# First attention of a two-layer network: scores a whole unit ahead, two blocks sharing a piece, key and query projections joined

## The chip, the core and the metric

The kernel runs on one core of a Trainium2 chip. The core has a matmul engine (TensorE, PE in the profile), three engines for elementwise work (VectorE or DVE, ScalarE or ACT, GpSimd or POOL) and a queue engine (SyncE or SP) that issues DMAs here. All of them run their own instruction streams and meet only at semaphores. The metric is the time of one execution on the device, in microseconds (us); smaller is better.

## What is computed

The reference is a network of two layers on an input x of 8 batch entries, 512 positions and 256 features, all in float32. Each layer is x + mixer(norm(x)) * silu(feed-forward(norm(x))). The change lies in the mixer of the first layer, a causal attention with linear biases: 16 heads of keys and values, two query heads to each, 64 features a head.

```python
qkv = inputs @ W_qkv
q = ...reshape(B, S, 32, 64)            # two query heads for each of the 16 key heads
k, v = ...reshape(B, S, 16, 64), each repeated for its two query heads
bias = ALIBI_SLOPES[:, None, None] * (pos[None, :] - pos[:, None])
scores = einsum('bhqd,bhkd->bhqk', q, k) / sqrt(64) + bias
scores = where(pos_q >= pos_k, scores, -inf)
attn = softmax(scores, axis=-1)
out = einsum('bhqk,bhkd->bhqd', attn, v).reshape(B, S, 2048)
return out @ W_out
```

The feed-forward part, the second layer (a recurrence, another attention, routed experts) and the norms are not touched.

## The kernel before

The whole is one program. `layernorm_phase` comes first and `head_attention_phase` after it (it takes the stretch from about 55 to 1515 us), then the first layer's feed-forward network, the recurrence, the second attention, the routing and the experts. Only `head_attention_phase` is changed.

Its work is cut into units. A unit is one batch entry (B = 8) of one key head (KVH = 16) with its two query heads, so there are 128 units; `t` counts them, and `par` is `t` modulo 2. The 512 positions are four blocks of 128 (TT = 4). By causality, block qt of the queries needs qt + 1 blocks of keys, so scores are 128, 256, 384 or 512 wide. Products in full precision are made of operands split into a high and a low part, in three terms (high by high, low by high, high by low).

PE's work for a unit, with its function and line:

- `project` (L970): six matmuls of 512 columns over 128 rows for keys and values together (`project_kv`), and six for the two query heads (`project_q`), into the banks `m_ps`.
- `turn_v` (L986): four small transposes of v.
- `score` (L1031): for each block six matmuls over 64 rows, two heads side by side in two halves of the array, into the two banks `s_ps`.
- `turn` (L1042): for each block the transposes of the weights p, 4 (qt + 1) pieces over 64 rows, into two banks `t_ps`.
- `weigh` (L1052): the sum over v, 16 matmuls over 128 rows (the four blocks of keys, of 512, 384, 256 and 128 columns), into `o_ps`.
- `project_out` (L997): two times three matmuls of 512 columns (the halves m of the output), into `m_ps`.

The other engines, for each unit:

- DVE: `mask` (L894) adds the bias to a block's score of one head, u = 2 * block + head, takes it out of `s_ps` and finds the row's limit; `invert` (L900) takes reciprocals of the sums; `turn_out` (L905) copies half of the turned weights; `values` (L886) copies v; `k_rest` (L881), `q_rest` (L874) and `rest_o` (L916) compute the low parts; `add_out` (L912) adds the output to `acc`.
- ACT: `exps` (L815) the exponential of a block and head; `turn_out` (L821) the other half of the turned weights; `take_kv` (L808, L809), `take_q` (L801) and `take_o` (L827) the high parts.
- POOL: `scale` (L767) multiplies the exponentials by the reciprocals; once a head it splits new weights (L758, L760).
- SP: `copy_k` (L710) copies the split key by two DMAs of 256 KB each from `k_parts` (64 partitions) into both halves of `k_twice[par]`, and counts them in `k_copied[par]`.

The order is written out by hand in four functions called `body`, one for each engine, and in `body` of PE it is, for block qt of 0 to 3 in unit t:

1. `score` of the block that is three blocks ahead (AHEAD0 = 6 counts block and head, so qt = 0 scores block 3 of unit t, and qt = 1 to 3 score blocks 0 to 2 of unit t + 1); in its last term it waits until block qt of unit t has been scaled (`turnable`).
2. `turn(qt)`.
3. A piece of 128 rows: after qt = 0 `turn_v` of unit t + 1 and `weigh` of unit t - 1; after qt = 1 `project_kv` of unit t + 2; after qt = 2 `project_out` of unit t - 1; after qt = 3 `project_q` of unit t + 2.

DVE, ACT and POOL follow the same blocks. The waits that PE's `body` makes are put where a matmul of the piece before still runs. The key copy of unit t + 1 is waited for in `weigh` of body t (`operands`); it comes from the projection in body t - 1. The low part of the attention's output is waited for in `project_out` (`o_low`), one piece and a block after `weigh`.

Of the kernel before, what the change touches and what calls it, by code (L numbers as in the profile page):

```python
# [597 lines left out]
def head_attention_phase(nc, w_heads, wo_heads, slopes, ident, xh, xl, acc, xh_dram, xl_dram, row_sb, coef_sb,  # L598
# [9 lines left out]
    with ExitStack() as ctx:  # L608
# [65 lines left out]
        AHEAD0 = 6  # L674
# [4 lines left out]
        def ahead(t, qt):  # L679
            return (t, 2 * qt + AHEAD0) if qt < TT - AHEAD0 // 2 else (t + 1, 2 * qt + AHEAD0 - 2 * TT)  # L680

        def soon(t, qt):
            return (t, qt + 2) if qt + 2 < TT else (t + 1, qt + 2 - TT)
# [4 lines left out]
        def q_count(n):  # L688
            return n * 5
# [4 lines left out]
        def out_count(n, m):  # L694
            return n * 5 + (13 + m)
# [53 lines left out]
        def _(pool):  # L749
# [12 lines left out]
            def scale(t, qt):  # L762

                wait_alone(pool, recips, t * TT + (qt + 1), pool_ticks)
                for u in (2 * qt, 2 * qt + 1):
                    p = p_sb[:, u, 0:(qt + 1) * P]
                    pool.tensor_scalar(p, p, recip[:, u:u + 1], 1.0, ALU.mult, ALU.mult).then_inc(scaled, 1)  # L767

            def body(t):
                for qt in range(TT):  # L770
                    scale(*soon(t, qt))
# [5 lines left out]
            with pool.Fori(0, KVH // 2) as jj:  # L777
                for jp in range(2):
# [3 lines left out]
                    pool.wait_ge(proj, j * (5 * B) + out_count(-1, 1))  # L782
# [14 lines left out]
        def _(act):  # L797
# [13 lines left out]
            def exps(n, u):  # L811

                N = (u // 2 + 1) * P
# [4 lines left out]
            def turn_out(n, qt, par):  # L818

                act.wait_ge(turned, n * TT + (qt + 1))  # L820
                act.activation(pT[par][:, :, 0:qt + 1, qt * P + HD:qt * P + P], turned_half(1)[:, :, 0:qt + 1, :],  # L821
                               ACT.Copy).then_inc(odd_out, 1)
# [10 lines left out]
            for u in range(AHEAD0):  # L833
                exps(0, u)
            with act.Fori(0, KVH * B // 2) as pair:
                for par in range(2):
                    t = pair * 2 + par
                    for qt in range(TT):
                        n, u = ahead(t, qt)
                        if qt == 0:  # L840
                            take_q(q_count(t + 1), 1 - par)
                        exps(n, u)
                        turn_out(t, qt, par)
                        exps(n, u + 1)
                        if qt == 0:
                            take_o(t, 1 - par)
                        if qt == 1:
                            take_kv(kv_count(t + 2), par, pair + par)
            take_o(KVH * B, 1)
            take_q(q_count(KVH * B + 1), 1)  # L850

        @block.vector
        def _(dve):
# [35 lines left out]
            def mask(n, u):  # L889


                N = (u // 2 + 1) * P
                wait_alone(dve, scored, n * 8 + (u + 1), dve_ticks)
                dve.tensor_tensor_reduce(out=p_sb[:, u, 0:N], in0=s_ps[u % 2][:, 0:N],  # L894
# [3 lines left out]
            def invert(n, qt):  # L898
                dve.wait_ge(exped, n * 8 + (2 * qt + 2))
                dve.reciprocal(recip[:, 2 * qt:2 * qt + 2], total[:, 2 * qt:2 * qt + 2]).then_inc(recips, 1)  # L900

            def turn_out(n, qt, par):

                dve.wait_ge(turned, n * TT + (qt + 1))
                dve.tensor_copy(pT[par][:, :, 0:qt + 1, qt * P:qt * P + HD], turned_half(0)[:, :, 0:qt + 1, :])\  # L905
# [12 lines left out]
            def body(t, par, b_before, new_head=None):  # L918

                for qt in range(TT):  # L920
                    n, u = ahead(t, qt)
                    if u == 0 and new_head is not None:

                        dve.wait_ge(masked, t * 8 + 10)
                        set_bias(new_head, False, new_head * 2 + 2)
                    if qt == 3:
                        add_out(t + (-1), 1 - par, b_before, 0)
                    if qt == 0:
                        q_rest(t + 1, 1 - par)
                    mask(n, u)  # L930
                    invert(*soon(t, qt))
                    mask(n, u + 1)
                    turn_out(t, qt, par)
                    if qt == 1:
                        values(v_count(t + 1), 1 - par)
                        rest_o(t, 1 - par)
                    if qt == 2:
                        k_rest(t + 2, par)
                    if qt == 3:
                        add_out(t + (-1), 1 - par, b_before, 1)  # L940
# [6 lines left out]
            for u in range(AHEAD0):  # L947
                mask(0, u)
# [8 lines left out]
            q_rest(KVH * B + 1, 1)  # L957
            rest_o(KVH * B, 1)

            for m in range(KT):  # L960
                add_out(KVH * B - 1, 1, B - 1, m, skipped=2)

        @block.tensor
        def _(pe):
            def project(bank, w, b):

                terms = [(wh, xh), (wl, xh), (wh, xl)]
                for i, (weight, x) in enumerate(terms):
                    for k in range(KT):
                        ins = pe.matmul(bank[:], weight[:, k, w:w + P], x[:, k, ds(b * S, S)],  # L970
# [3 lines left out]
            def project_q(n, par, b):  # L974

                pe.wait_ge(proj_out, q_count(n) + (-2))
                project(m_ps[1 - par], 0, b)

            def project_kv(n, par, b):
                pe.wait_ge(proj_out, kv_count(n) + (-2))  # L980
                project(m_ps[par], P, b)
# [1880 lines left out]
```

## Time and profile before

| | us |
|---|---|
| median of three runs | 3470.98 |
| lowest, highest | 3469.5, 3473.81 |
| the profiled execution, its own time | 3471.95 |
| its span in the trace | 3470.2 |
| PE busy in the span | 3213.3 (93%) |
| DVE, ACT, POOL busy | 2348.2 (68%), 2064.0 (59%), 1184.7 (34%) |
| granted TensorE clock over the span, share of full | 0.96 |

The page of the profile gives busy times and the costliest groups. The timeline gives instructions in order of time, and neighbours of a kind merged to one row: the start, the length from there to the end of the last, the engine, the line, the operation, output<-inputs, the shape and the count. An idle note in brackets tells how long the engine was idle before the row, and what it waited for. As matmuls are pipelined, a row's length reaches into the next row, so the time that a piece holds PE is read from its start to the start of the next piece. PEld is PE's loading of weights, which can run beside a matmul. Each operand of a matmul is written as rows*columns.

### The profile page before, as it was taken

The numbers are of one execution on the slowest core, as the hardware profiler recorded it, in microseconds if no ns is written. First come the engines' busy times: TensorE is split into PE (matmuls) and PEld (weight loads), VectorE is DVE, ScalarE is ACT, GpSimd is POOL, SyncE is SP. The second block draws the span as 40 slices with busy tenths as digits, with TensorE's granted clock in tenths as the row PEclk, the third lists the DMA queues.
The fourth block names the chain that finished last, engine by engine and source line by source line (L and its number), as shares of the span: only waits on it lengthen the run. The fifth ranks groups of instructions, "written<-read, shape, count | busy, mean of one in ns | idle before, by whom it ended". The sixth has DMA issues, their size and how long they took to land. (4 is left out here: it accounts for less than half of the span.)

```text
span 3470.2 us, 74087 instructions
## 1 busy us (share of the span) xinstructions
PE 3213.3 (93%) x22696; PEld 2398.4 (69%) x22696; DVE 2348.2 (68%) x6849; ACT 2064.0 (59%) x4943; POOL 1184.7 (34%) x1818
## 2 busy tenths in 40 slices
PE   4999999999999999989999979979999964999995
PEld 3777777676777677768888865546666653888884
DVE  5888887887888788776666655556666626666664
ACT  4777777777777777765555543236566621555553
POOL 4434344444333434443333320042321202334432
PEclk9999999999999999999999999969999967999998
DMA  3222222222222222243333331111111134445545
GB/s 95 59 54 59 52 51 57 59 58 54 59 59 54 58 59 57 55 136 121 131 127 127 133 121 49 39 40 28 32 28 27 27 123 148 118 125 143 128 120 164
DMA packets 175948, 280.43 MB, mean 81 GB/s; under 512 B 32850, under 2 KB 117586, under 8 KB 175826
## 3 DMA queue, kind: packets, MB, share of 16 engines
q1 hardware_dynamic: 161234, 258.94, 26.1%
q0 software_dynamic: 14592, 19.93, 3.5%
q8 instruction: 69, 1.13, 0.1%
q14 instruction: 53, 0.43, 0.0%
HBM read 159.79 MB, written 41.16 MB: 58 GB/s over the span
## 5 line engine op out<-in xcount | busy, mean ns | idle before, releaser
L767 POOL TENSOR_SCALAR at_p<-at_p,at_recip 128x128 f32<-128x128 f32 (+3 forms) x1028 | 533.6, 532 | 868.0 <-DVE at_recip L900 868.0
L815 ACT ACTIVATE at_p<-at_p,at_nmax 128x128 f32<-128x128 f32 (+3 forms) x1030 | 573.6, 557 | 336.4 <-DVE at_nmax L894 324.7
L894 DVE CUSTOM_DVE_ANT_0 at_p<-at_s_ps,at_bias 128x128 f32<-128x128 f32 (+3 forms) x1030 | 497.3, 483 | 208.5 <-PE at_s_ps L1031 199.7
L1031 PE MATMUL at_s_ps<-at_k_twice,at_q 64*128 64x128 f32 (+3 forms) x3090 | 379.4, 350 | 5.2 <-DVE at_nmax L894 4.2
L1860 DVE CUSTOM_DVE_ANT_0 aa_a_ps<-aa_a_ps,aa_hidden 128x128 f32<-128x128 f32 (+3 forms) x512 | 247.2, 507 | 173.6 <-PE aa_a_ps L2024 170.8
L1031 PEld LDWEIGHTS at_s_ps<-at_k_twice,at_q 64*128 64x128 f32 x3090 | 232.2, 185 | 176.7 <-issue 162.7
L1052 PE MATMUL at_o_ps<-at_pT,at_v 128*64 128x512 f32 (+3 forms) x2064 | 306.8, 439 | 0.0
L1760 ACT ACTIVATE aa_pT<-aa_b_ps 128x512 f32<-128x512 f32 (+1 forms) x384 | 196.6, 529 | 175.9 <-PE aa_b_ps L2042 173.1
L526 DVE SCALAR_TENSOR_TENSOR nw_hl<-nw_h,nw_coef_now,nw_hh 128x512 fp32r<-128x512 f32 x192 | 149.8, 780 | 163.1 <-ACT nw_hh L454 163.1
L449 ACT ACTIVATE nw_h<-nw_h_ps,nw_b 128x512 f32<-128x512 f32 x192 | 132.1, 688 | 211.1 <-PE nw_h_ps L553 210.6
L905 DVE COPY at_pT<-at_t_ps 128x128 f32<-128x128 f32 (+3 forms) x512 | 248.9, 486 | 0.0
L1042 PE MATMUL at_t_ps<-ident,at_p 64*128 64x64 f32 x5120 | 245.5, 222 | 0.0
L1042 PEld LDWEIGHTS at_t_ps<-ident,at_p 64*128 64x128 f32 x5120 | 229.2, 138 | 16.8 <-issue 0.2
L1052 PEld LDWEIGHTS at_o_ps<-at_pT,at_v 128*64 128x64 f32 x2064 | 137.1, 137 | 147.7 <-issue 119.7
L2575 POOL DMA_INDIRECT moe_dram<-ex_o,places x76 | 124.7, 1641 | 304.0 <-ACT ex_o L2602 212.1
L821 ACT ACTIVATE at_pT<-at_t_ps 128x128 f32<-128x128 f32 (+3 forms) x512 | 216.0, 422 | 3.1
L391 POOL TENSOR_SCALAR nw_w1h<-nw_w_raw 128x256 fp32r<-128x256 f32 x192 | 104.2, 543 | 324.0 <-PE nw_o_ps L568 318.4
L2024 PE MATMUL aa_a_ps<-aa_k,aa_q 128*128 128x128 f32 (+3 forms) x512 | 191.1, 386 | 14.9 <-DVE aa_nmax L1860 11.3
L970 PE MATMUL at_m_ps<-xh,at_wh 128*128 128x512 f32 (+1 forms) x520 | 190.0, 447 | 12.4 <-POOL at_wl L760 11.9
L815 ACT ACTIVATION_READ_ACCUMULATOR at_p<-at_p,at_nmax 128x1 f32 x1030 | 194.2, 189 | 0.0
L2614 ACT ACTIVATE ex_act<-ex_a_ps 128x512 f32<-128x512 f32 x114 | 68.1, 598 | 185.8 <-PE ex_b_ps L2710 179.0
L912 DVE TENSOR_TENSOR acc<-at_m_ps,acc 128x512 f32 (+1 forms) x258 | 174.6, 677 | 1.8 <-PE at_m_ps L997 1.8
(317 smaller groups left out, 7942.7 us busy)
## 6 DMA issues: line engine op xcount, KB each, us to landing
at_k_twice<-at_k_parts SPq DMA_DIRECT2D x260, 256.0 KB, 3.7
w_raw<-in_w_dram SPq DMA_DIRECT2D x57, 768.0 KB
nw_w_raw<-in_w_all_dram SPq DMA_DIRECT2D x26, 1024.0 KB, 5.0
nw_w_raw<-in_w_all_dram SPq DMA_DIRECT2D x52, 512.0 KB, 6.8
nw_xh<-xh_dram SPq DMA_DIRECT2D x10, 512.0 KB, 4.3
nw_xl<-xl_dram SPq DMA_DIRECT2D x10, 512.0 KB, 4.9
at_w_raw<-in_w_heads_dram SPq DMA_DIRECT2D x18, 256.0 KB, 4.4
nw_x<-in_x_dram SPq DMA_DIRECT2D x9, 512.0 KB, 5.9
```

The costliest lines, as they stand in the source:

```text
L767: pool.tensor_scalar(p, p, recip[:, u:u + 1], 1.0, ALU.mult, ALU.mult).then_inc(scaled, 1)
L815: act.activation(p_sb[:, u, 0:N], p_sb[:, u, 0:N], ACT.Exp, bias=nmax[:, u:u + 1], scale=-1.0, accum_out=total[:, u:u + 1]).then_inc(exped, 1)
L821: act.activation(pT[par][:, :, 0:qt + 1, qt * P + HD:qt * P + P], turned_half(1)[:, :, 0:qt + 1, :], ACT.Copy).then_inc(odd_out, 1)
L894: dve.tensor_tensor_reduce(out=p_sb[:, u, 0:N], in0=s_ps[u % 2][:, 0:N], in1=bias[:, u % 2, S - N:S], scale=1.0, scalar=BIG, op0=ALU.add, ...
L905: dve.tensor_copy(pT[par][:, :, 0:qt + 1, qt * P:qt * P + HD], turned_half(0)[:, :, 0:qt + 1, :])\
L970: ins = pe.matmul(bank[:], weight[:, k, w:w + P], x[:, k, ds(b * S, S)], start=(i == 0 and k == 0), stop=(i == 2 and k == KT - 1))
L1031: ins = pe.matmul(s_ps[h][:, 0:N], qst[par][rows, q, at], k_twice[par][rows, k, 0:N], start=(i == 0), stop=(i == 2))
L1042: ins = pe.transpose(turned_half(half)[:, h, k, :], p_sb[rows, 2 * qt + h, k * P:k * P + P], ident[rows, rows])
L1052: ins = pe.matmul(o_ps[HD * h:HD * h + HD, k * P:S], v[par][:, k, :], pT[par][:, h, k, k * P:S], start=(k == 0), stop=(k == TT - 1))
L1760: act.activation(pT[group_of(n, s) % 2][:, s % REP, piece * S:piece * S + N], b_ps[done % 3][:, 0:N], ACT.Exp, scale=-1.0)\
L1860: dve.tensor_tensor_reduce(out=a_ps[i % 2][:, 0:N], in0=a_ps[i % 2][:, 0:N], in1=hidden[:, S - N:S], scale=1.0, scalar=BIG, op0=ALU.add, o ...
L2024: pe.matmul(a_ps[i % 2][:, 0:N], q_all[n % 2][:, head // 2, N - P:N], k_all[n % 2][:, head % 2, g, 0:N], start=True, stop=True).then_inc(s ...
```

## The change

PE's body has a new order, and the blocks are numbered anew: j = 0 is block 3, j = 1 to 3 are blocks 0 to 2 (`block_of`). `p_sb`, `nmax`, `total` and `recip` are indexed by j, and so are masks, exponentials and scalings.

- All scores that body t makes are of unit t + 1 ("a whole unit ahead"); before, block 3 was of unit t. The setup before the loop scores all four blocks of unit 0, and takes the query of unit 1.
- Blocks 0 and 1 are turned one after the other and then scored one after the other. Their scores share a bank: block 0 in its columns 0 to 128, block 1 in 128 to 384 (`score_at`); the turned pieces share one likewise (`turned_at`). DVE waits for both (`scored`, 6; `turned`, 3).
- `project_kv` and `project_q` of unit t + 2 follow each other. The waits have moved into them (`last`, ahead of the third term).
- `project_out` does half 1 first, then half 0, and holds at its last matmul the waits for the next body, the copy of unit t + 2's key among them (`next_unit`).
- ACT, DVE and POOL follow the new order. On DVE `k_rest`, `rest_o` and `q_rest` now stand one behind the other, ahead of `turn_out` of block 2.

The core of the diff:

```diff
+        def block_of(j):
+            return (j + TT - 1) % TT
...
+        def score_at(j):
+            first = P if block_of(j) == 1 else 0
+            return slice(first, first + (block_of(j) + 1) * P)
+
+        def soon(t, j):
+            return (t, j + 2) if j + 2 < TT else (t + 1, j + 2 - TT)
...
         def _(act):
...
+                    turn_out(t, 0, par)
+                    exps(t + 1, 0)
+                    exps(t + 1, 1)
+                    turn_out(t, 1, par)
+                    turn_out(t, 2, par)
+                    take_o(t, 1 - par)
+                    exps(t + 1, 2)
+                    exps(t + 1, 3)
+                    exps(t + 1, 4)
+                    take_kv(kv_count(t + 2), par, pair + par)
+                    exps(t + 1, 5)
+                    take_q(q_count(t + 2), par)
+                    turn_out(t, 3, par)
+                    exps(t + 1, 6)
+                    exps(t + 1, 7)
...
         def _(dve):
...
+                if new_head is not None:
+
+                    dve.wait_ge(masked, t * 8 + 10)
+                    set_bias(new_head, False, new_head * 2 + 2)
+                turn_out(t, 0, par)
+                mask(t + 1, 0)
+                mask(t + 1, 1)
+                invert(*soon(t, 0))
+                turn_out(t, 1, par)
+                turn_out(t, 2, par)
+                values(v_count(t + 1), 1 - par)
+                for u in range(2, 6):
+                    mask(t + 1, u)
+                invert(*soon(t, 1))
+                invert(*soon(t, 2))
+                k_rest(t + 2, par)
+                rest_o(t, 1 - par)
+                q_rest(t + 2, par)
+                turn_out(t, 3, par)
+                mask(t + 1, 6)
+                mask(t + 1, 7)
+                invert(*soon(t, 3))
+                add_out(t + (-1), 1 - par, b_before, 1)
+                add_out(t + (-1), 1 - par, b_before, 0)
...
         def _(pe):
...
+            def turnable(n, before, upto):
+                pe.wait_ge(even_out, n * TT + (before + 1))
+                pe.wait_ge(odd_out, n * TT + (before + 1))
+                pe.wait_ge(scaled, n * 8 + 2 * upto)
...
+                def next_turnable():
+                    turnable(t, 3, 4)
+                    pe.wait_ge(o_low, t + 1)
+
+                def next_unit():
+                    turnable(t + 1, 0, 1)
+                    pe.wait_ge(k_copied[par], half * 32 + 64)
+
+                turn(0)
+                score(t + 1, 1 - par, 0, lambda: values_free(t + 1))
+                turn_v(t + 1, 1 - par)
+                weigh(t + (-1), 1 - par, lambda: turnable(t, 1, 3))
+                turn(1)
+                turn(2)
+                score(t + 1, 1 - par, 1)
+                score(t + 1, 1 - par, 2)
+                if new_head is not None:
+
+                    pe.wait_ge(w_split, new_head + 1)
+                project_kv(t + 2, par, b_next, lambda: pe.wait_ge(proj_out, v_count(t + 1)))
+                project_q(t + 2, par, b_next, next_turnable)
+                turn(3)
+                score(t + 1, 1 - par, 3)
+                if new_out is not None:
+
+                    pe.wait_ge(wo_split, new_out + 1)
+                project_out(t + (-1), 1 - par, lambda: pe.wait_ge(proj_out, q_count(t + 2)), next_unit)
```

In `project_out` the loop runs over m = 1, 0; `bank_free` stands ahead of m = 0 and `last` ahead of its third matmul. In the loop's head `half` is `t` divided by 2.

## Rows read from the trace of the kernel before

**Rows 1.** The page: span, and busy time by engine.

```profile
span 3470.2 us, 74087 instructions
...
PE 3213.3 (93%) x22696; PEld 2398.4 (69%) x22696; DVE 2348.2 (68%) x6849; ACT 2064.0 (59%) x4943; POOL 1184.7 (34%) x1818
```

**Rows 2.** Stretch: length; busy of PE, PEld, DVE, ACT, POOL; granted clock; DMA share; GB/s.

```profile
120.00:1500.00 1380.00, 1380.00 (x12519) 970.38 (x12516) 1109.03 (x3712) 1022.75 (x2946) 557.04 (x1045) 1.00 0.25 57
```

**Rows 3.** Timeline of PE, one unit: start us, length us, line, output<-inputs.

```profile
799.97 0.80 PE L1031 MATMUL at_s_ps<-at_k_twice,at_q 64*128 64x384 f32 x6
800.60 0.66 PE L1042 MATMUL at_t_ps<-ident,at_p 64*128 64x64 f32 x16
801.19 0.73 PE L970 MATMUL at_m_ps<-xh,at_wh 128*128 128x512 f32 x2
...
802.79 0.96 PE L1031 MATMUL at_s_ps<-at_k_twice,at_q 64*128 64x512 f32 x6
...
804.05 2.37 PE L1052 MATMUL at_o_ps<-at_pT,at_v 128*64 128x512 f32 x16
806.35 0.55 PE L1031 MATMUL at_s_ps<-at_k_twice,at_q 64*128 64x128 f32 x6
...
807.10 0.72 PE L970 MATMUL at_m_ps<-xh,at_wh 128*128 128x512 f32 x2
...
808.69 0.62 PE L1031 MATMUL at_s_ps<-at_k_twice,at_q 64*128 64x256 f32 x6
809.15 0.53 PE L1042 MATMUL at_t_ps<-ident,at_p 64*128 64x64 f32 x12
809.61 0.50 PE L997 MATMUL at_m_ps<-at_oh,at_woh 128*128 128x512 f32 x1
...
810.42 0.40 PE L997 MATMUL at_m_ps<-at_oh,at_woh 128*128 128x512 f32 x1
...
810.89 0.40 PE L997 MATMUL at_m_ps<-at_ol,at_woh 128*128 128x512 f32 x1
811.21 0.61 PE L1031 MATMUL at_s_ps<-at_k_twice,at_q 64*128 64x384 f32 x3
```

**Rows 4.** Timeline of PE's weight loads, same unit.

```profile
801.53 0.42 PEld L970 LDWEIGHTS at_m_ps<-xh,at_wl 128*128 128x128 f32 x2
...
808.69 0.41 PEld L1031 LDWEIGHTS at_s_ps<-at_k_twice,at_q 64*128 64x128 f32 x6 [0.37 <-issue]
```

**Rows 5.** Timeline of all engines, same unit: the links of the chains.

```profile
803.24 0.58 ACT L801 ACTIVATE at_q<-at_m_ps 128x512 fp32r<-128x512 f32 x1
...
803.85 0.69 DVE L874 SCALAR_TENSOR_TENSOR at_q<-at_m_ps,at_q 128x512 fp32r<-128x512 f32 x1 [0.60 <-ACT at_q L801]
...
805.07 0.16 DVE L900 RECIPROCAL at_recip<-at_total 128x2 f32<-128x2 f32 x1
...
805.43 1.14 POOL L767 TENSOR_SCALAR at_p<-at_p,at_recip 128x384 f32<-128x384 f32 x2 [1.45 <-DVE at_recip L900]
...
808.89 0.59 ACT L808 ACTIVATE at_k_parts<-at_m_ps 64x512 fp32r<-64x512 f32 x1 [0.32 <-PE at_m_ps L970]
...
809.49 0.42 DVE L894 CUSTOM_DVE_ANT_0 at_p<-at_s_ps,at_bias 128x256 f32<-128x256 f32 x1 [0.50 <-PE at_s_ps L1031]
...
810.72 0.67 DVE L881 TENSOR_TENSOR at_k_parts<-at_m_ps,at_k_parts 64x512 fp32r<-64x512 f32 x1
...
811.42 0.46 SPq L710 DMA_DIRECT2D at_k_twice<-at_k_parts  x1
```

**Rows 6.** Instructions of tile at_k_twice, whole run: landing of its DMAs.

```profile
DMA to landing us min/median/max: 2.9/3.7/4.7
```

**Rows 7.** Groups by line and shape, 120 to 1500 us: count, busy us, mean ns.

```profile
L767 POOL TENSOR_SCALAR at_p<-at_p,at_recip 128x256 f32<-128x256 f32 x246 | 114.9, 480 | 260.1 <-DVE at_recip L900 260.1
```

**Rows 8.** Busy time by stretch, columns as in rows 2: two stretches with pauses.

```profile
62.00:68.00 6.00, 2.07 (x17) 1.57 (x18) 1.88 (x9) 3.15 (x10) 0.00 (x0) 0.89 0.29 62
...
2890.00:2917.00 27.00, 15.46 (x115) 14.63 (x113) 14.52 (x10) 0.00 (x0) 13.64 (x7) 1.00 0.04 12
```

More of the change, by code:

```diff
@@ L688, in q_count @@
         def q_count(n):
[L689 removed]
+            return n * 5 + (-2)
         def v_count(n):
@@ L832, in _ @@
             take_kv(4, 1, 0)
-            for u in range(AHEAD0):
+            take_q(5, 1)
+            for u in range(2 * TT):
                 exps(0, u)
@@ L918, in body @@
             def body(t, par, b_before, new_head=None):
[L920 to L940, printed above, removed]
+                if new_head is not None:
[21 more added lines that the diff above has]
+                add_out(t + (-1), 1 - par, b_before, 0)
             set_bias(0, True, 2)
@@ L946, in _ @@
             k_rest(1, 1)
-            for u in range(AHEAD0):
+            q_rest(1, 1)
+            for u in range(2 * TT):
                 mask(0, u)
@@ L956, in _, with project @@
                 body(j * B + (B - 1), 1, B - 2, new_head=j + 1)
-            q_rest(KVH * B + 1, 1)
             rest_o(KVH * B, 1)
-            for m in range(KT):
-                add_out(KVH * B - 1, 1, B - 1, m, skipped=2)
+            for m in (1, 0):
+                add_out(KVH * B - 1, 1, B - 1, m, skipped=3)
         @block.tensor
         def _(pe):
-            def project(bank, w, b):
+            def project(bank, w, b, last=None):
                 terms = [(wh, xh), (wl, xh), (wh, xl)]
@@ L969, in project @@
                     for k in range(KT):
+                        if i == 2 and k == 0 and last is not None:
+                            last()
                         ins = pe.matmul(bank[:], weight[:, k, w:w + P], x[:, k, ds(b * S, S)],
@@ L987, in turn_v, with project_out @@
                 ins.then_inc(proj, 1)
-            def project_out(n, par, skipped=0):
-                pe.wait_ge(o_low, n + 2)
-                for m in range(KT):
+            def project_out(n, par, bank_free, last):
+                for m in (1, 0):
                     bank = m_ps[2 if m else par]
-                    pe.wait_ge(proj_out, out_count(n, m) + (-5 if m else -2 - skipped))
+                    if m == 0:
+                        bank_free()
                     for i, (w, o) in enumerate([(woh, oh), (wol, oh), (woh, ol)]):
+                        if m == 0 and i == 2:
+                            last()
@@ L1022, in score @@
+            def score(n, par, j, late=None):
+                u, qt = 2 * j, block_of(j)
+                at = slice(qt * P, qt * P + P)
+                N = (qt + 1) * P
+                if j != 2:
+                    pe.wait_ge(masked, n * 8 + (u + 2))
                 for i, (q, k) in enumerate([(0, 0), (1, 0), (0, 1)]):
-                    if i == 1 and between is not None:
-                        between()
                     if i == 2 and late is not None:
-                        turnable(*late)
-                        if late[1] == 0:
-                            turned_out(late[0] + (-1))
+                        late()
@@ L1091, in _ @@
             pe.wait_ge(k_copied[0], 32)
-            for u in range(0, AHEAD0, 2):
-                score(0, 0, u)
-            pe.wait_ge(proj_out, 4)
+            for j in range(TT):
+                score(0, 0, j)
+            pe.wait_ge(proj_out, 5)
+            pe.wait_ge(k_copied[1], 32)
+            pe.wait_ge(even_out, 1)
+            pe.wait_ge(odd_out, 1)
+            pe.wait_ge(scaled, 2)
             with pe.Fori(0, KVH) as j:
```

128 lines of the change are left out of this document (40 added, 88 removed).

## The prediction

> **What bounds the kernel now.** I read the page first: TensorE (PE) is busy for 93% of the span, DVE for 68% [rows 1]. The table by stretches then says that from 120 to 1500 us PE is busy for 1380.00 of 1380.00 us at a granted clock of 1.00 (2.4 GHz), DVE for 1109 and ACT for 1023 [rows 2]. As a busy PE can hide small losses, I read its timeline from start to start of the pieces. One unit (one batch entry of one head, 128 in all) goes from 799.97 to 811.21, 11.24 us, and no row of it has an idle note [rows 3]. PE never waits here; its own work sets the time. So two things are asked of the change: what it takes off PE, and whether the other engines still deliver in time.
>
> PE's work has a price beside its columns. Two steps of an output matmul take 0.47 (810.42 to 810.89), so one is 0.235, and six are 1.41; but the six of the key projection hold PE for 1.59, from 807.10 to 808.69 [rows 3]. The other 0.18 lies at the two ends, where PE changes between operands of 64 rows (scores, turns) and of 128. Inside a piece the next weights are loaded under the matmul before; behind a change the load starts together with its matmul, at 808.69, after 0.37 us without a load [rows 4]. A unit has eight changes: four blocks of score and turn, and four pieces of 128 rows (weigh, key, output, query).
>
> **What the change takes off PE.** Six changes are left. Key and query lie end to end: 0.18 less. Blocks 0 and 1 are turned together and scored together, so a block of 64 rows has gone with its entry and exit. The entry costs 0.10 (809.61 to 810.42 is 0.81 for three steps of 0.235, the same change). The exit costs 0.07 (sixteen turned pieces take 0.59 and twelve 0.46, thus 0.0325 each and 0.07 over) [rows 3]. No column is added. The unit on PE is 11.24 - 0.35 = 10.89 us, and 128 x 0.35 = 45 us is the whole gain to be had.
>
> The new order from the rows, with 0 at the first matmul of turn(0): turn block 3, score block 3, turn v are 0.59 + (1.26 - 0.13) - 0.07 = 1.65 (0.13 for block 0's four turned pieces); weigh 2.30, to 3.95; turn 0 and 1, score 0 and 1 are 0.13 + 0.75 + 0.46 - 0.10 = 1.24, to 5.19. There the key projection begins; call it V. Key and query 1.59 + 1.60 - 0.18 = 3.01; turn and score of block 2 are 0.46 + 0.63 = 1.09, to V + 4.10; output 1.60, to V + 5.70 = 10.89 [rows 3].
>
> Here the Trainium skill has a rule, in TensorE: Matmul & The Clock Gate, section Part 3 (What overlaps and what doesn't): a weight load overlaps a running matmul only when its row group differs. The loads at 801.53 go to the rows of the matmul before and hide under it all the same [rows 4]; the trace doesn't agree. By that rule a change of rows would cost nothing of its own, and the gain on PE would be 0 instead of 45 us.
>
> **What it puts in: three waits on chains that are too short.** "A unit ahead" holds for the scores. But the key of unit t+2 is still projected in body t, and next_unit() makes PE wait at the last matmul of body t for that key's copy by DMA. Before, the copy had to be there in the weigh of body t+1, some 8 us of PE later.
>
> (a) The copy of the key. From the first key matmul to ACT's first activation it is 808.89 - 807.10 = 1.79 us, and ACT had waited for just that. The two activations last 0.59 each, end to start. DVE starts 0.03 behind a result of ACT that it waits for (803.24 + 0.58 to 803.85). k_rest takes 0.67, and SP issues 0.03 behind it (811.42) [rows 3, 5]. Ahead of take_kv ACT now has the exponentials of u = 2 to 4, whose masks stand behind two copies and the values on DVE; they end at about V + 1.9, 0.1 later than 1.79. So: ACT at V + 1.9, vT_out at V + 3.1, the residue whole at V + 3.8, first issue there. The second DMA goes out 0.55 later (its first issue lasts 0.46), and a landing takes 3.7 in the median (2.9 to 4.7) [rows 6]: V + 8.1. PE's own work reaches that wait, the weights of the last output matmul, at V + 5.70 - 0.32 - 0.235 = V + 5.15. It stands for 2.95 us, less 0.1, since a load set free starts its matmul at once. That costs 2.85.
>
> The skill's page DMA: Bandwidth & Descriptors, section Anatomy of one DMA, gives for another path of issue 2.0 us plus bytes at 436 GB/s. By it the two copies (512 KB) would take an estimated 3.2 and not 4.25 us, and the sum would be some 100 us lower; no row shows so short a time for both.
>
> (b) next_turnable(), at the fifth matmul of the query, waits for o_low of this body. On DVE rest_o now stands behind k_rest, which waits for vT_out: k_rest at V + 3.1, rest_o 0.6 later with 0.67, o_low at V + 4.4 [rows 5]. PE is there at V + 1.41 + 0.94 - 0.235 = V + 2.1 and stands for 2.3. Behind that wait on PE are all of turn 3, score 3 and the output; behind k_rest on DVE are q_rest, a copy, two masks and two adds. This doesn't add to (a): PE comes to the copy's wait at about V + 7.4 instead of 5.15, and the copy holds it 0.7 more. It is the floor where the copy is quick.
>
> (c) weigh's last block waits until block 1 of the same unit (j = 2) is scaled. The reciprocal for it stands on DVE behind two masks of the 512-wide score. That score starts at 0.55. The 256-wide one is answered by DVE 0.80 after its start (808.69 to 809.49, waited for); this one lasts 0.3 longer (the 384-wide piece is 0.17 longer than the 256-wide): mask at 1.6. Two masks of some 0.6 (DVE's 512-wide pass, as in k_rest) and the reciprocal, 0.16: 3.0. POOL starts 0.20 later (805.07 + 0.16 to 805.43) and scales two of 0.48: 4.2 [rows 3, 5, 7]. PE wants it at 3.95 - 0.32 = 3.6: 0.6 us of waiting.
>
> A cycle is 10.89 + 0.6 + 2.85 = 14.35 us against 11.24: 3.1 more. Does another engine make more of that? DVE has, after the query's high part (by (b) at V + 5.9), q_rest 0.6, a copy 0.5, two masks 1.0, a reciprocal 0.1, two adds 1.2: free at V + 9.3. The next turn(0) begins at V + 8.5 and its block can be copied 0.8 later. It just fits. The output's second bank is wanted at V + 7.1 and is free at V + 6.6.
>
> Bounds. (a): landings of 2.9 and 4.7 give -0.8 and +1.0, but downward only 0.7, as (b) is next. (c): 0, if the scaling is hidden, or 1.2, if DVE's last add is late. I take the middle, because each link has a row of its own kind. set_bias, two of some 0.6 us on DVE per head, was under DVE's idle time and now stands ahead of (c): half of it, 15 x 0.6 = 9 us, between 0 and 18. Splitting the weights goes into POOL's idle time (POOL is busy for 557 of 1380 us [rows 2]); were it not, 2 us a head, 30 us. The start scores one block more, the end keeps its chain: 3 us, between -3 and 6. All else of the kernel is as before: 0.
>
> Sum, against the profiled execution's 3471.95 us: + 128 x 3.1 = 397, + 9, + 3 = 3881. The median of the runs shown is 1 less: 3880.
>
> **The rivals.**
> 1. Faster: PE never stands, 3471 - 45 = 3426. It needs a landing by V + 5.15. Before, with the same links, 807.10 to 811.42 and 4.25 were 8.6 [rows 3, 5, 6]. For it speaks only that the wait might mean an earlier copy; but k_copied[par] >= half * 32 + 64 counts in unit t+2's. 3%. Losses that just cancel 45 us: 1%.
> 2. Shorter chains: the copy quick, so (b) decides, and (c) hidden: 14.35 - 0.7 - 0.6 = 13.05 a unit, 3715. 13%.
> 3. DVE's tail decides: q_rest is late, and adds, copy and the masks of (c) slide by 0.6 a unit: 3957; with landings of 4.7 some 4030. It does so once the tail ends over 0.8 after turn(0) starts. 13%.
> 4. The clock falls. PE would be busy for some 75%, with pauses up to 2.3 us. From 2890 to 2917 it was busy for 57% at a granted clock of 1.00; from 62 to 68 for 34%, and there the clock fell (0.89 in the mean) [rows 8]. At 1.2 GHz the 5.8 us up to V and much behind it nearly double, some 20 us a unit: about 4600. 5%.
> The forecast has 65%.
>
> **How the numbers follow.** Predicted 3880; its own range, half the bounds above, 3800 to 3960. To hold 8 in 10 I take 3740 to 4000: the forecast, most of rivals 2 and 3, not the clock and not the faster case. Less than 0.2% can't be told from no change. Faster 0.03, same 0.01, slower 0.96.
>
> **What would show it.** PE's timeline of a unit: 14.4 us, with idle ahead of weigh's last block (released by POOL), at the query's third term (DVE at_ol) and at the last output matmul (DMA at_k_twice); PE busy for some 75% of the stretch; key and query with no gap between. I am wrong if PE stays above 95% there, if a landing comes before V + 7, or if the granted clock drops.

## The result

| | before | changed |
|---|---|---|
| median, us | 3470.24 | 3950.99 |
| lowest, highest | 3466.83, 3473.81 | 3947.59, 3952.39 |
| the profiled execution, its own time | 3471.95 | 3947.59 |
| ratio, 95% interval | | 1.1381 (1.1364 to 1.1398) |

The change makes the kernel 13.8% slower, 481 us. That is the side that was forecast, and inside the range of 3740 to 4000; the forecast itself, 3880, is 71 us too low.

The page of the changed kernel, against [rows 1]:

```profile
span 3945.8 us, 72670 instructions
...
PE 3346.0 (85%) x22702; PEld 2407.5 (61%) x22702; DVE 2371.7 (60%) x6853; ACT 2091.5 (53%) x4947; POOL 1180.4 (30%) x1818
```

The span has grown by 475.6 us, while no engine has more work to speak of: DVE 2372 us against 2348, and PE six matmuls more. PE's busy time is 133 us higher all the same, because at a lower clock each matmul lasts longer, and because the modelled end of a matmul is counted into each wait that follows it (in the unit shown below PE is busy for 11.64 us). The table by stretches, with the columns of [rows 2]; the first row answers to the row there, the others are two pieces of it:

```profile
120.00:1900.00 1780.00, 1460.08 (x12179) 947.84 (x12178) 1100.52 (x3609) 1018.59 (x2864) 536.71 (x1015) 0.94 0.19 43
912.90:925.20 12.30, 9.93 (x98) 6.54 (x98) 7.05 (x24) 7.68 (x22) 4.00 (x8) 1.00 0.22 57
925.20:928.60 3.40, 3.40 (x20) 2.32 (x22) 2.91 (x9) 1.31 (x4) 1.12 (x3) 0.51 0.32 69
```

PE is busy for 82% of the first attention instead of all of it, and its granted clock is 0.94 in the mean: mostly 1.00, but for some 230 us in all about half of that, as from 925.2 to 928.6. Such a stretch is called a fall below.

Now PE's timeline of one unit in which the clock doesn't fall, cut to the rows that carry it. It begins with turn(0) at 972.91, and the next one at 987.32, 14.41 us later:

```profile
972.91 0.75 PE L1048 MATMUL at_t_ps<-ident,at_p 64*128 64x64 f32 x16
...
974.59 2.15 PE L1058 MATMUL at_o_ps<-at_pT,at_v 128*64 128x512 f32 x12
977.18 0.44 PE L1058 MATMUL at_o_ps<-at_pT,at_v 128*64 128x128 f32 x4 [0.44 <-POOL at_p L773]
977.55 0.59 PE L1048 MATMUL at_t_ps<-ident,at_p 64*128 64x64 f32 x12
...
978.82 0.73 PE L987 MATMUL at_m_ps<-xh,at_wh 128*128 x2
...
983.35 0.69 PE L987 MATMUL at_m_ps<-xl,at_wh 128*128 x2 [1.94 <-POOL at_p L773]
...
986.89 0.50 PE L1013 MATMUL at_m_ps<-at_ol,at_woh 128*128 128x512 f32 x1 [0.39 <-DMA at_k_twice<-at_k_parts]
987.32 0.46 PE L1048 MATMUL at_t_ps<-ident,at_p 64*128 64x64 f32 x8
```

Three waits stand where the prediction put them: 0.44 us ahead of weigh's last block, 1.94 at the query's third term, 0.39 at the last output matmul. A note of this kind is smaller than what a wait takes, because a matmul's modelled end reaches over the next start: weigh goes from 974.59 to 977.55, 2.96 us, where before it held PE for 2.30 [rows 3], so the first wait takes 0.66. The third is named after DMA at_k_twice. The second has POOL beside it, but POOL's scaling of block 2 was over by 981.9; the last to come was DVE's rest_o (982.53 and 0.67, thus 983.20), and in 75 of 119 units the wait is put down to DVE at_ol.

The chain in the same unit, all engines, to be held against [rows 5]:

```profile
973.11 0.69 DVE L924 TENSOR_TENSOR acc<-at_m_ps,acc 128x512 f32 x1 [0.49 <-PE at_m_ps L1013]
...
973.73 0.69 DVE L917 COPY at_pT<-at_t_ps 128x512 f32<-128x512 f32 x1
...
976.20 0.93 POOL L773 TENSOR_SCALAR at_p<-at_p,at_recip 128x256 f32<-128x256 f32 x2 [3.57 <-DVE at_recip L911]
...
980.71 0.57 ACT L814 ACTIVATE at_k_parts<-at_m_ps 64x512 fp32r<-64x512 f32 x1
...
981.30 0.59 ACT L815 ACTIVATE at_vT<-at_m_ps 64x512 f32<-64x512 f32 x1
...
981.92 0.68 DVE L892 TENSOR_TENSOR at_k_parts<-at_m_ps,at_k_parts 64x512 fp32r<-64x512 f32 x1 [1.32 <-ACT at_vT L815]
...
982.53 0.67 DVE L928 TENSOR_TENSOR at_ol<-at_o_ps,at_oh 128x512 fp32r<-128x512 f32 x1
982.63 1.10 SPq L716 DMA_DIRECT2D at_k_twice<-at_k_parts  x2
```

### The profile page after: what moved, and what is told of

Same layout as the page of the kernel before. It is cut to its first block and busy times, and to the rows that moved or that the text cites. A ratio compares the mean times of both kernels' runs of the same rounds, so it can differ in the third digit from the quotient of the medians.

```text
span 3945.8 us, 72670 instructions
## 1 busy us (share of the span) xinstructions
PE 3346.0 (85%) x22702; PEld 2407.5 (61%) x22702; DVE 2371.7 (60%) x6853; ACT 2091.5 (53%) x4947; POOL 1180.4 (30%) x1818
## 3 DMA queue, kind: packets, MB, share of 16 engines
q8 instruction: 69, 1.13, 0.1%
## 5 line engine op out<-in xcount | busy, mean ns | idle before, releaser
L773 POOL TENSOR_SCALAR at_p<-at_p,at_recip 128x512 f32<-128x512 f32 (+3 forms) x1028 | 530.3, 531 | 1352.0 <-DVE at_recip L911 1352.0
L821 ACT ACTIVATE at_p<-at_p,at_nmax 128x512 f32<-128x512 f32 (+3 forms) x1032 | 571.5, 554 | 342.4 <-DVE at_nmax L905 339.1
L905 DVE CUSTOM_DVE_ANT_0 at_p<-at_s_ps,at_bias 128x512 f32<-128x512 f32 (+3 forms) x1032 | 462.6, 488 | 30.1 <-PE at_s_ps L1036 23.9
L917 DVE COPY at_pT<-at_t_ps 128x512 f32<-128x512 f32 (+3 forms) x512 | 237.4, 485 | 289.2 <-PE at_t_ps L1048 285.5
L987 PE MATMUL at_m_ps<-xl,at_wh 128*128 128x512 f32 (+1 forms) x520 | 178.7, 425 | 249.3 <-DVE at_ol L928 155.6
L1036 PE MATMUL at_s_ps<-at_k_twice,at_q 64*128 64x512 f32 (+3 forms) x3096 | 361.2, 354 | 4.7 <-DVE at_nmax L905 4.4
L828 ACT ACTIVATE at_pT<-at_t_ps 128x512 f32<-128x512 f32 (+3 forms) x512 | 210.2, 436 | 272.5 <-PE at_t_ps L1048 272.2
L987 PEld LDWEIGHTS at_m_ps<-xl,at_wh 128*128 128x128 f32 x520 | 89.5, 192 | 314.3 <-POOL at_p L773 151.1
L1036 PEld LDWEIGHTS at_s_ps<-at_k_twice,at_q 64*128 64x128 f32 x3096 | 236.3, 196 | 11.5 <-DVE at_nmax L905 5.0
L885 DVE SCALAR_TENSOR_TENSOR at_q<-at_m_ps,at_q 128x512 fp32r<-128x512 f32 x130 | 89.9, 691 | 200.2 <-ACT at_q L807 200.2
L892 DVE TENSOR_TENSOR at_k_parts<-at_m_ps,at_k_parts 64x512 fp32r<-64x512 f32 x130 | 88.7, 683 | 188.5 <-ACT at_vT L815 188.5
```

The costliest lines, as they stand in the source:

```text
L821: act.activation(p_sb[:, u, 0:N], p_sb[:, u, 0:N], ACT.Exp, bias=nmax[:, u:u + 1], scale=-1.0, accum_out=total[:, u:u + 1]).then_inc(exped, 1)
L1036: ins = pe.matmul(s_ps[h][:, score_at(j)], qst[par][rows, q, at], k_twice[par][rows, k, 0:N], start=(i == 0), stop=(i == 2))
```

## The experiments

All of them are edits of the changed kernel, and their ratios are to the kernel before on the same chip. The kernel before took 3470.1 to 3475.4 us in the median from one chip to the next, so a difference of a few us between two experiments is read from the ratios and the traces. A unit's length is read from the start of one weigh to the start of the next.

### rest_o ahead of k_rest (no_b)

```diff
-                k_rest(t + 2, par)
                 rest_o(t, 1 - par)
+                k_rest(t + 2, par)
```

> On DVE rest_o stands ahead of k_rest, so PE's wait for o_low is met early. Theory A (the key's copy decides, and the wait for o_low lies inside it): PE's pause at the query shrinks to some 1 us (the scaling of block 2 ends at about V + 3.0), the one at the last output matmul grows from 0.7 to some 2 us, a unit stays at 14.4 where the clock doesn't fall, and the time stays within 30 us of 3951. Theory B (the two waits add up): 1.3 us less a unit, 3785.

Measured: 3962.56 us, ratio 1.1403 (1.1384 to 1.1422). PE's waits in a unit of 14.39 us without a fall of the clock:

```profile
1012.90 0.44 PE L1058 MATMUL at_o_ps<-at_pT,at_v 128*64 128x128 f32 x4 [0.45 <-POOL at_p L773]
...
1017.55 0.72 PE L987 MATMUL at_m_ps<-xl,at_wh 128*128 128x512 f32 x2 [0.43 <-POOL at_p L773]
...
1022.61 0.50 PE L1013 MATMUL at_m_ps<-at_ol,at_woh 128*128 128x512 f32 x1 [1.87 <-DMA at_k_twice<-at_k_parts]
```

The wait at the query has shrunk from 1.94 to 0.43 and the one at the copy has grown from 0.39 to 1.87. The time has moved by 12 us only, and upward: the two waits lie one inside the other, and the copy decides.

### Another key, no wait for the copy (no_a), and both (no_ab)

```diff
-                ins = pe.matmul(s_ps[h][:, score_at(j)], qst[par][rows, q, at], k_twice[par][rows, k, 0:N],
+                ins = pe.matmul(s_ps[h][:, score_at(j)], qst[par][rows, q, at], k_twice[0][rows, k, 0:N],
...
-                    pe.wait_ge(k_copied[par], half * 32 + 64)
+                    pe.wait_ge(k_copied[1 - par], (half + par) * 32 + 32)
```

The copies in the loop all go to `k_twice[1]`, which no score reads.

> All scores in the loop read the first unit's key, and the copies go to a buffer that nobody reads, so the wait for the copy of unit t+2's key is replaced by that for unit t+1's, long met (the scores are therefore those of another key; every instruction stays). Theory A: the wait for o_low is the floor, 0.7 us less a unit than before, 14.2 in the mean: 3860. Theory B (the copy alone holds the kernel): the unit falls to about 11.5, 3515.

> Both: the first unit's key in all scores, and rest_o ahead of k_rest. Theory A: what is left is 10.9 of PE's work, 0.6 for the scaling ahead of weigh's last block and some 1.0 for the scaling of block 2 at the query: 12.5 us a unit, 3640. Theory B (DVE's order is the bound as soon as the copy isn't): above 13.5 us a unit, over 3770.

Measured: no_a 3921.9 us, ratio 1.1284 (1.1261 to 1.1306); no_ab 3675.39 us, ratio 1.0575 (1.0554 to 1.0596). PE's waits in a unit of no_a (13.72 us), then in one of no_ab (12.65 us):

```profile
860.77 0.44 PE L1058 MATMUL at_o_ps<-at_pT,at_v 128*64 128x128 f32 x4 [0.44 <-POOL at_p L773]
...
866.95 0.69 PE L987 MATMUL at_m_ps<-xl,at_wh 128*128 x2 [1.95 <-DVE at_ol L928]
```

```profile
732.58 0.44 PE L1058 MATMUL at_o_ps<-at_pT,at_v 128*64 128x128 f32 x4 [0.70 <-POOL at_p L773]
...
737.42 0.70 PE L987 MATMUL at_m_ps<-xl,at_wh 128*128 x2 [0.62 <-POOL at_p L773]
```

Without the copy's wait the chain behind o_low is indeed the floor: 1.95 us at the query, and the last output matmul doesn't wait. Units without a fall come to 13.7 to 14.0 us, where 0.7 less than 14.4 was expected; but half of the units still have a fall, and take 15.45 us in the median, so the time went down by 29 and not by 91 us. In the changed kernel all 63 units without a fall wait for the copy, and of the 65 with one only 8 do, so a fall there is paid in part out of the copy's wait; without that wait it costs some 1.5 us. With both waits gone, a unit takes 12.64 us in the median, for the 12.5 expected, and the kernel 3675 us, for 3640 (one unit in eight, the last of a head, takes 1.4 us more than the others). The wait at the query is then put down to POOL's scaling, as expected; the prediction doesn't name this chain, and no run takes it away by itself. The copy is not alone in holding the kernel: without it a unit would be 11.5 by theory B, and it is 13.7.

### Block 1's reciprocal ahead of the masks (no_c, no_abc)

```diff
+                invert(*soon(t, 0))
                 turn_out(t, 0, par)
                 mask(t + 1, 0)
                 mask(t + 1, 1)
-                invert(*soon(t, 0))
```

> On DVE the reciprocal for block 1 stands ahead of the copy and the two 512-wide masks. Theory A (the wait ahead of weigh's last block is in series with the copy's chain): PE's pause there goes, 0.5 us less a unit, 3885, give or take what the clock's falls do. Theory B (the slack is taken up by the copy's wait): no change, 3951.

> The first unit's key in all scores, rest_o ahead of k_rest, and block 1's reciprocal ahead of the masks. Theory A: 0.5 us less a unit than with the first two (12.64), so 12.1, and 3610; what is left above 10.9 is the scaling of block 2 at the query. Theory B (something else than the scaling holds the last 1.2 us): PE's pause is not at the query.

Measured: no_c 3839.69 us, ratio 1.1071 (1.1054 to 1.1088); no_abc 3542.9 us, ratio 1.021 (1.0191 to 1.0228). PE's waits in a unit of no_c (13.66 us), then in one of no_abc (11.77 us):

```profile
819.34 0.70 PE L987 MATMUL at_m_ps<-xl,at_wh 128*128 x2 [1.95 <-POOL at_p L773]
...
822.83 0.51 PE L1013 MATMUL at_m_ps<-at_ol,at_woh 128*128 128x512 f32 x1 [0.34 <-DMA at_k_twice<-at_k_parts]
```

```profile
684.16 0.70 PE L987 MATMUL at_m_ps<-xl,at_wh 128*128 x2 [0.62 <-POOL at_p L773]
```

The wait in weigh is gone and the other two are what they were (1.95 and 0.34): it stands in series with the copy's chain, as the prediction has it. The unit falls from 14.40 to 13.7, by the 0.66 that the wait took, not by the 0.5 that I had read from its note. That is 85 to 90 us; about 20 more came with the clock, which falls in 37 of 128 units instead of 65. Nothing but one wait of 0.62 is left in no_abc. It is 67 us faster than expected (3610), and its unit 11.7 us and not 12.1, for the same reason: the wait that it takes away was noted at 0.70 in no_ab and took 0.9.

### The pause filled with work (fill8)

```diff
                 def next_turnable():
+                    for _ in range(8):
+                        pe.matmul(m_ps[2][:], wh[:, 0, 0:P], xh[:, 0, ds(b_next * S, S)], start=True, stop=True)
                     turnable(t, 3, 4)
```

> Eight more 512-wide matmuls on PE ahead of the waits in the query's third term (into a bank that nobody reads then): 1.7 us of work laid into a pause of 1.9 us, once a unit. Theory A (the changed kernel took 70 us more than its chains because the granted clock fell for 3.4 us in half of the units): with the pause filled the falls go, every unit takes 14.4 us instead of 14.92 in the mean, and the kernel gets faster by 50 to 70 us, to about 3885. Theory B (the units of 15.2 us come from DVE's tail or from longer landings, and the falls only go with them): 3951 or a little more, since PE has more work.

Measured: 3904.48 us, ratio 1.1238 (1.1219 to 1.1257). More work on PE, and 47 us less, a little under the 50 to 70 expected. The table by stretches, as above, and PE's timeline in a unit of 14.31 us:

```profile
120.00:1900.00 1780.00, 1643.15 (x13418) 1096.77 (x13419) 1116.19 (x3685) 1040.29 (x2926) 551.72 (x1036) 1.00 0.20 44
```

```profile
756.48 2.03 PE L1066 MATMUL at_m_ps<-xh,at_wh 128*128 128x512 f32 x8
758.60 0.70 PE L987 MATMUL at_m_ps<-xl,at_wh 128*128 128x512 f32 x2
...
762.07 0.49 PE L1013 MATMUL at_m_ps<-at_ol,at_woh 128*128 128x512 f32 x1 [0.31 <-DMA at_k_twice<-at_k_parts]
```

The eight matmuls run from 756.48 to 758.60, where PE stood before, and the granted clock is 1.00 over the whole attention. The unit without a fall is as long as it was (14.41 in the median against 14.40), so the pause cost its own length and a second thing, the clock. In the changed kernel PE's rows show that second price; output matmuls that are 0.235 apart elsewhere:

```profile
925.57 0.63 PE L1013 MATMUL at_m_ps<-at_oh,at_wol 128*128 128x512 f32 x1
926.00 0.63 PE L1013 MATMUL at_m_ps<-at_ol,at_woh 128*128 128x512 f32 x1
```

0.43 us apart, and a unit with such a fall mostly takes 15.2 us. (The rows lie in the stretch of 925.20 to 928.60 above.) 65 of the 128 units have one. The 129 weighs begin between 77.07 and 1986.77 us in the changed kernel and between 77.36 and 1945.99 in this one, so the mean unit is 14.92 and 14.60 us: 0.32 x 128 = 41 us are the clock's.

### Without the new head's bias (fill8_nobias)

```diff
-                    set_bias(new_head, False, new_head * 2 + 2)
+                    pass
```

> The changed kernel with the pause at the query filled, and without a new bias at a head's end (all heads take the first head's bias, so the computation differs in that; two passes of 0.64 us on DVE are gone, once a head). Theory A (the one unit in eight that takes 15.85 instead of 14.42 us is that of the bias, now with its full length on the chain ahead of weigh's last block): 16 x 1.3 = 21 us less than with the filled pause alone, 3883. Theory B (it is the split weights or the DMAs at the head's end): no change, 3904.

Measured: 3896.15 us, ratio 1.1227 (1.1208 to 1.1246): 8 us less than with the bias (4 by the ratios, as the two ran on different chips), between the two theories, and the intervals overlap. The trace says more than the times. With the filled pause, one unit in eight, the last of a head, takes 15.85 us in the mean and the others 14.42; without the bias it takes 15.20. So 0.65 of the 1.43 us are the bias and 0.78 are something else. The rows of fill8 at a head's end, then the last wait of such a unit in fill8_nobias:

```profile
767.44 0.44 PE L1058 MATMUL at_o_ps<-at_pT,at_v 128*64 128x128 f32 x4 [1.16 <-POOL at_p L773]
...
772.90 1.10 SPq L716 DMA_DIRECT2D at_k_twice<-at_k_parts  x2
...
778.07 0.47 PE L1013 MATMUL at_m_ps<-at_ol,at_woh 128*128 128x512 f32 x1 [1.29 <-DMA at_k_twice<-at_k_parts]
```

```profile
775.21 0.47 PE L1013 MATMUL at_m_ps<-at_ol,at_woh 128*128 128x512 f32 x1 [1.27 <-DMA at_k_twice<-at_k_parts]
```

The wait in weigh is noted at 1.16 instead of 0.45: that is the bias. The copy's wait is 1.29 instead of 0.31, with the bias or without, and the copy takes from 772.90 to 778.07, 5.17 us; in the changed kernel's unit above it took from 982.63 to 986.89, 4.26. Over all of fill8 it is 4.29 in the median in the middle of a head and 5.11 in the 16 units at a head's end. There SP sends the spill (774.37) and the next weights (775.43, 776.30) right behind the copy. That these slow it is argued from the order in time; no run takes them away.

### Six pieces with the scores two blocks ahead (lead2, lead2_s, lead2_b, lead2_sb)

This keeps the change's six pieces and takes the three waits away. PE's body becomes:

```diff
                 turn(0)
-                score(t + 1, 1 - par, 0, lambda: values_free(t + 1))
+                score(t, par, 3, lambda: values_free(t + 1))
                 turn_v(t + 1, 1 - par)
-                weigh(t + (-1), 1 - par, lambda: turnable(t, 1, 3))
+                weigh(t + (-1), 1 - par, operands)
                 turn(1)
                 turn(2)
-                score(t + 1, 1 - par, 1)
-                score(t + 1, 1 - par, 2)
+                score(t + 1, 1 - par, 0, lambda: pe.wait_ge(proj_out, t * 5 + 7))
...
                 turn(3)
-                score(t + 1, 1 - par, 3)
+                score(t + 1, 1 - par, 1)
+                score(t + 1, 1 - par, 2, lambda: pe.wait_ge(o_low, t + 1))
```

`operands` holds the wait for the copy of unit t + 1's key, beside `turnable(t, 1, 3)`. DVE takes the reciprocals of blocks 0 and 1 around its first copy, adds the output one body later, behind the masks of block 2, and has rest_o ahead of k_rest; ACT and POOL follow.

> The six pieces stay, but the scores are two blocks ahead instead of four (block 2 of the unit, then block 3, then blocks 0 and 1 of the next), the key's copy is waited for in weigh of the next body, block 1's reciprocal stands ahead of the masks, and the output is added one body later. Theory A (the six pieces save 0.35 us of PE's work a unit, and only the three waits hid it): a unit of 10.9 us and PE without pause, 3425. Theory B (with six pieces DVE and ACT have too few and too uneven breaks, and PE waits for them whatever the lead): over 11.24 a unit, 3470 or more. Theory C (a change of rows costs nothing in itself): 3470, with PE always busy.

Measured: 3478.4 us, ratio 1.0024 (1.0015 to 1.0033). That is 53 us above theory A. A unit takes 11.12 us, one in each head 12.25. I read the missing 0.2 us as a price of the order inside a block, and tried that:

```diff
+                score(t + 1, 1 - par, 0, lambda: pe.wait_ge(proj_out, t * 5 + 7))
                 turn(1)
                 turn(2)
-                score(t + 1, 1 - par, 0, lambda: pe.wait_ge(proj_out, t * 5 + 7))
...
+                score(t + 1, 1 - par, 1)
+                score(t + 1, 1 - par, 2, lambda: pe.wait_ge(o_low, t + 1))
                 turn(3)
-                score(t + 1, 1 - par, 1)
-                score(t + 1, 1 - par, 2, lambda: pe.wait_ge(o_low, t + 1))
```

On DVE `values`, which now waits until weigh is through, and the masks of block 3 then stand ahead of the copies of blocks 0 and 1.

> As the version with scores two blocks ahead, but in its second and third block of 64 rows PE scores first and turns after, the order that the kernel before has everywhere. Theory A (a score straight behind turned pieces pays 0.09 us, since its first weights aren't loaded ahead, and three such places took back most of what six pieces save): two places less, 0.16 us less of PE a unit, 11.12 to 10.95, and 3458. Theory B (the order within a block is free, and the 0.25 us over the rows of before come from waits): 3478, no change.

Measured: 3446.02 us, ratio 0.9919 (0.9906 to 0.9933), the fastest kernel here, 0.8% below the one before. A unit takes 10.89 us. PE's timeline of lead2, then of lead2_s:

```profile
809.96 0.58 PE L1049 MATMUL at_t_ps<-ident,at_p 64*128 64x64 f32 x12
...
811.23 0.73 PE L988 MATMUL at_m_ps<-xh,at_wh 128*128 128x512 f32 x2
...
814.23 0.59 PE L1049 MATMUL at_t_ps<-ident,at_p 64*128 64x64 f32 x12
...
815.49 0.50 PE L1014 MATMUL at_m_ps<-at_oh,at_woh 128*128 128x512 f32 x1
...
817.14 0.71 PE L1049 MATMUL at_t_ps<-ident,at_p 64*128 64x64 f32 x16
...
818.44 0.40 PE L1002 MATMUL at_m_ps<-ident,at_vT 64*128 64x64 f32 x4
```

```profile
779.57 2.37 PE L1060 MATMUL at_o_ps<-at_pT,at_v 128*64 128x512 f32 x16
781.88 0.97 PE L1038 MATMUL at_s_ps<-at_k_twice,at_q 64*128 64x512 f32 x6
...
783.15 0.73 PE L989 MATMUL at_m_ps<-xh,at_wh 128*128 128x512 f32 x2
...
786.15 0.96 PE L1038 MATMUL at_s_ps<-at_k_twice,at_q 64*128 64x128 f32 x12
...
787.41 0.50 PE L1015 MATMUL at_m_ps<-at_oh,at_woh 128*128 128x512 f32 x1
...
789.00 0.71 PE L1050 MATMUL at_t_ps<-ident,at_p 64*128 64x64 f32 x16
...
790.13 0.40 PE L1003 MATMUL at_m_ps<-ident,at_vT 64*128 64x64 f32 x4
790.47 2.37 PE L1060 MATMUL at_o_ps<-at_pT,at_v 128*64 128x512 f32 x16
```

The time came down, but not for the reason I gave. The second block of 64 rows takes 809.96 to 811.23 = 1.27 with the turns first and 781.88 to 783.15 = 1.27 with the score first; the third 814.23 to 815.49 = 1.26 and 786.15 to 787.41 = 1.26. The order is free. What shrank is the first block, whose order is the same in both: 817.14 to 818.44 = 1.30 against 789.00 to 790.13 = 1.13. Its score waits for the masks of blocks 0 and 1, and in lead2 DVE gives the last of them just then:

```profile
806.01 0.71 PE L1049 MATMUL at_t_ps<-ident,at_p 64*128 64x64 f32 x16
...
806.20 0.42 DVE L902 CUSTOM_DVE_ANT_0 at_p<-at_s_ps,at_bias 128x256 f32<-128x256 f32 x1
...
806.68 0.80 PE L1037 MATMUL at_s_ps<-at_k_twice,at_q 64*128 64x384 f32 x6
```

The mask of 806.20 is through at 806.6, and PE's score starts at 806.68, 0.67 after the turns began; PE's row has no idle note, because the last turned pieces reach to it. The wait takes some 0.15 us: in lead2_s the score starts 0.53 after the turns (789.53). Scored first, blocks 0 and 1 come to DVE 0.4 us earlier; DVE's own order was changed with it, and no run separates the two. Another 0.06 us lie in the output (815.49 to 817.14 against 787.41 to 789.00), where lead2's second half waits for q_rest on DVE. Theory B of lead2_s had the cause right (waits) and its time wrong.

> As the version with scores two blocks ahead, but DVE makes a new head's bias right behind the last mask of the old one, ahead of the two adds, where it has a break. Theory A (the unit of 12.25 us, one in each head, comes from the bias, 1.3 us on DVE ahead of the masks and the query's rest): that unit falls to some 11.4, 16 x 0.8 = 13 us less, 3465. Theory B (it comes from POOL's splitting of the weights or from the DMAs at a head's end): no change.

> Both of them: score first in two blocks, and the bias early. By theory A of each, 20 and 13 us less: 3445, below the kernel before by 0.7%. If DVE or ACT becomes the bound once PE's unit is under 11.1, it stays above 3460.

```diff
                 mask(t, 7)
+                if new_head is not None:
+
+                    dve.wait_ge(masked, t * 8 + 10)
+                    set_bias(new_head, False, new_head * 2 + 2)
                 add_out(t + (-2), par, b_before, 1)
```

Measured: lead2_b 3474.74 us, ratio 1 (0.999 to 1.0009); lead2_sb 3448.23 us, ratio 0.9923 (0.9909 to 0.9936). The bias moved gains little: the long unit goes from 12.25 to 11.95 us, where 11.4 was expected, and the mean unit from 11.26 to 11.23, 4 us in all (8 by the ratios, for the 13 expected). Now the score of block 3 waits for the two adds behind the bias:

```profile
787.41 0.50 PE L1037 MATMUL at_s_ps<-at_k_twice,at_q 64*128 64x512 f32 x2 [0.48 <-DVE acc L921]
```

Which place would cost nothing stays open; beside lead2_s it gains nothing. That lead2_sb came out at the 3445 expected is luck: lead2_s gave all of it, for another reason, and the bias none.

## Why the prediction was right, point by point

The side and the mechanism were right: three waits of the length and at the places forecast, two in series and one hidden. The forecast of 3880 fell 71 us short, inside the stated range, because one rival that it had put aside, the clock, came true in part. By its own list of signs it was wrong there: it named a drop of the granted clock as one of them.

- **What bounds the kernel; PE's own work.** Right. 10.89 us a unit for six pieces is what lead2_s takes in the median to the hundredth (779.57 to 790.47 is 10.90). The gain of 45 us is there once nothing waits: lead2_s is 29 us below the kernel before, and its mean unit is 10.99 and not 10.89 (one in each head takes 11.8), which is 13 us, and its first weigh begins 2.4 us later. The rule of the Trainium skill (TensorE: Matmul & The Clock Gate, section Part 3 (What overlaps and what doesn't)), by which a load overlaps a running matmul only in another row group, would have made that gain 0. lead2_s speaks against the rule as it stands, with 0.8% less time and 0.35 us less a unit for the same columns.
- **(a) the copy's chain.** With V = 978.82: ACT at V + 1.89 (forecast 1.9), k_rest at V + 3.10 (3.1), the DMA out at V + 3.81 (3.8), PE free at V + 8.07 (8.1).
- **(b) o_low.** rest_o is through at V + 4.38 (4.4), PE goes on at V + 4.53. That it hides inside (a) is shown by no_b, that it is the floor by no_a. What the prediction left out here is POOL's scaling of block 2, which the same `next_turnable` waits for: hidden in the changed kernel, it stands for a noted 0.62 us once both other chains are gone (no_ab, no_abc).
- **(c) the scaling.** With 0 = 972.91: POOL at 3.29 (3.2), PE free at 4.27 (4.2), a wait of 0.66 (0.6). Its being in series is shown by no_c.
- **A cycle** of 14.41 us where the clock stays, against 14.35: + 8 us.
- **The heads' ends.** 9 us were given to the bias. Its own part was right (0.65 x 16 = 10), but the copy lands 0.8 us later there, where the spill and the weights follow it: fill8's long unit gives 16 x 1.43 = 23, + 14 us. The bound for landings (4.7) had it, the sum took the median for all.
- **The clock.** This is the step that failed. Rival 4 was put as all or nothing, against a stretch that was busy for 57% at a clock of 1.00 [rows 8], and got 5% and nothing in the sum. What happens lies between: falls of mostly 3.4 us in half of the units, each costing some 0.6 us (41 us over 65). fill8 shows that they go when the pause at the query is filled with work, and that they cost 41 us. They don't need a pause at that place: in no_b the long one stands at the copy, and the falls are there too.
- **Start and end.** 77.07 against 72.44 for the first weigh, and 0.6 at the end: 5 us, for 3.

Forecast + 409, and + 8 + 14 + 41 + 2 make 474; the profiled execution took 475.6 more. All the misses have the same sign. PE was busy for 82% and not for some 75%; its work alone, 10.89 of 14.41 us, is 76%, and the rest is the modelled ends that reach into the waits, and the lower clock.

Some of the prediction's numbers on its bounds don't follow from its own terms. Half of the upper bounds is about 110 to 125 us, so the inner range would end near 4000 and not at 3960. Rival 2 at 3715 lies outside the range of 3740 to 4000 that is said to hold most of it. Rival 3 with landings of 4.7 adds 128 x 1.0 to 3957, about 4085 and not 4030. The measured 3951 lies inside with either set of numbers.

Rival 3 (DVE's tail decides) was not what made the time long: DVE's copy of the first turned block starts 0.82 after turn(0) (973.73), just behind the last add (973.11 and 0.6), against the 0.8 at which it could start: it just fits, as forecast. Of rival 2 (a quick copy, the scaling hidden) the changed kernel shows neither part.

## What to carry to other kernels

Before a piece is moved, take each result that it makes, and add up its chain to the first use from rows of the trace: here 8.1 us of ACT, DVE and DMA from the key projection to its copy, against 5.2 us of PE's work in the new order. "A unit ahead" in one operand (the scores) had brought the first use of another (the key) nearer to its making: before, its first score came 10.5 us behind the start of its projection (807.10 to 806.35 + 11.24 [rows 3]), and in the new order some 6.2. The two joins on PE together are worth a third of a microsecond a unit, and only in an order in which all chains still fit. Then price a new pause on PE twice, by its length and by what the clock does.

## What the hardware showed that I had not expected

- The granted clock fell to half, mostly for 3.4 us at a time, in 65 of 128 units, at a pause of about 2 us in each unit of 14.4 and PE busy for 82%. Filling the pause with eight matmuls whose result nobody reads took the falls away and made the kernel 47 us faster. With pauses of 0.4 and 1.9 (no_b) the clock is 0.94 in the mean as well; with 0.7 and 0.6 (no_ab) 7 units of 128 have a fall. In no_c 28 of the 37 falls lie in the first two units behind a head's end, where the copy's wait is noted at 1.25 us and not at some 0.4. Which feature of a pause decides, these runs don't show.
- The same two DMAs of 256 KB set PE going 4.3 us after the first issue in the middle of a head and 5.1 where three others follow them (fill8, medians of 111 and 16 units; without the bias 4.3 and 5.15).
- The idle notes of PE are smaller than what a wait takes by 0.2 us, and a short wait shows none at all (0.15 us in lead2).
